# The first gather pass of a two-layer graph network on Trainium2: one-hot rows built from slots that go through DRAM instead of through PE

## The chip, the cores and the metric

The kernel runs on one core of one Trainium2 chip. The metric is the device time of one execution in microseconds. Before the change the median of 3 runs is 19948.8 us (19933.13 to 19953.17).

## The reference, cut to what matters

There are 12500 nodes with 64 features and 412500 edges, sorted by `dst`. The first layer needs, for each edge, the distance between the rows of its two nodes, and the row of its target. What the first gather pass has to produce is, per edge, the product of two rows and their squares:

```python
h = mobius_matvec(weight, input, C)
dist = sqdist(h[edge[0]], h[edge[1]], C)[None, :]   # needs sum(x*y), sum(x*x), sum(y*y) per edge
edge_h = C / (C + dist)
h_e = logmap0(h, C)
...
e_rowsum = jax.ops.segment_sum(edge_e, edge[0], num_segments=N)[:, None]
h_prime = jax.ops.segment_sum(edge_e[:, None] * h_e[edge[1]], edge[0], num_segments=N)
```

`edge[0]` is `src` and `edge[1]` is `dst`. A second layer (edge network, batch norms, sums per node) follows and is not touched.

## The kernel before, in words

**Layout.** The edges are sorted by the kernel itself into tiles of 128, so that all edges of a tile have their `src` node in one chunk of 128 nodes (`ids` holds the chunk of each pair of tiles). A record of 8 floats per edge says the slot of the source node in its chunk (word 0), the target node (word 1) and the attributes. A block is TB = 16 tiles; there are NBLK = 214 blocks, NT = 3424 tiles. The sort (lines 344 to 616) ends with POOL scattering the records to DRAM (L602) while DVE ranks the edges (L495 flags, L503 scans, L508 copies).

**The first gather pass** (lines 754 to 938) works on each block as follows. `each_block` (L779) unrolls four blocks (`g`) in a hardware loop.
- SP loads the records of a block (L821), two buffers, two blocks ahead, after `rec_free` has been given twice: by POOL when it has the indices, and by DVE when it has the slots.
- ACT turns the target nodes into integer indices (`indices`, L848). It does so for block k+2 after the gathers of block k have landed (L851), and it writes the gathered rows to `rows_d` (L853).
- POOL issues 16 indirect DMAs a block (L839), each gathering 128 rows of 68 floats from `h0_d` into `G[g]`, of which there are four.
- The source rows come from a table `T0` in SBUF by a matmul with a one-hot matrix `OT` (slot against partition), per tile (L873). `T0` holds each row as three bf16 pieces of 64 and the three pieces of its square. `OT` needs the slot of each edge on every partition: DVE's `spread` (L900) multiplies the identity by the slots, giving the block's 16 diagonal matrices `DG`; PE's `broadcast` (L867) multiplies them by a matrix of ones into PSUM (`BC`, four banks); DVE's `onehot` (L908) compares `BC` with the partition's number.
- DVE adds the three pieces of the row sums out of PSUM (L919, twice a block, into `xrow` in SBUF) and of the squares (L921), multiplies `xrow` by the gathered rows (L926), copies three words per edge into `EDG` (L927) and sums the products (L930). Then `G[g]` is free.

The order is set by semaphores. The helpers are `consume(eng, s, n)` (L137), a wait followed by a subtraction, `hold` (L110), and `chunks_of` (L130), which loads eight chunk numbers into registers. DVE's order in a block is written out by hand: one-hots of the next block, spread of the one after, reduces, product, copies, sum.

**The second gather pass** (L681 in `gathers`, L689 in `onehots`, product L1359) comes later and isn't touched; it gathers as many rows, from `b_d`.

## Time and profile before

| | us |
|---|---|
| median of 3 runs | 19948.8 |
| the profiled execution's own time | 19907.3 |
| its span, first to last instruction | 19904.8 |
| POOL busy | 12116.0 (61%) |
| DVE busy | 7650.9 (38%) |
| PE busy | 6330.2 (32%) |
| ACT busy | 1873.1 (9%) |
| first gather pass, first to last gather | 5401.8 to 10336.6 |

The profile comes from one execution. Engines are PE (matmuls), PEld (weight loads), DVE (vector), ACT (scalar), POOL (GpSimd) and SP (which only issues DMAs). Busy time leaves out waiting and the issue of DMAs from SP and ACT; an indirect gather issued by POOL counts, since POOL works out its descriptors itself. A row "idle before, releaser" tells how long the engine stood before an instruction and what ended the wait; "issue" means that nothing in the profile was waited for. Lines are those of the kernel before.

### The profile page before, as it was taken

What the parts mean: (1) busy time and instruction counts of PE and PEld (TensorE: products, weight loads), DVE (VectorE), ACT (ScalarE), POOL (GpSimd) and SP (SyncE); (2) the same over time, 40 slices, a digit from 0 to 9 for tenths busy, and PEclk for the clock granted to TensorE, in tenths of its full rate; (3) what the DMA queues carried; (4) which work ended last, traced back from release to release, by engine and by line L of the source; (5) the groups of instructions that cost most, each with busy time, mean ns of one, the idle gap of its engine ahead of it and who ended that gap; (6) DMA issues with size and microseconds to landing.
All of it is one profiled execution on the core that took longest, in us unless ns stands there. A gap on an engine that the chain in (4) does not pass through costs nothing. (4 is left out here: it accounts for less than half of the span.)

```text
span 19904.8 us, 173884 instructions
## 1 busy us (share of the span) xinstructions
PE 6330.2 (32%) x43954; PEld 5014.5 (25%) x44061; DVE 7650.9 (38%) x16776; ACT 1873.1 (9%) x2728; POOL 12116.0 (61%) x12232
## 2 busy tenths in 40 slices
PE   0000000000021211212215744444444444458997
PEld 0000000000010110111105733333333333334885
DVE  5999000000144544544458861111111111226664
ACT  2000000000000000000000001111111111124333
POOL 0388777777677777777756735555555555530442
PEclk6555555555555555555558976666666666668998
DMA  1000000000012222222233311111111111155321
GB/s 49 3 3 2 5 5 5 5 5 5 18 50 52 51 51 53 50 52 50 52 39 98 121 57 40 41 41 40 42 40 41 41 40 42 40 87 189 94 93 54
DMA packets 678218, 917.93 MB, mean 46 GB/s; under 512 B 284316, under 2 KB 431387, under 8 KB 677916
## 3 DMA queue, kind: packets, MB, share of 16 engines
q0 software_dynamic: 322304, 245.26, 8.0%
q1 hardware_dynamic: 294236, 440.78, 7.2%
q10 hardware_dynamic: 61632, 231.44, 3.0%
q14 instruction: 36, 0.29, 0.0%
q8 instruction: 10, 0.16, 0.0%
HBM read 648.03 MB, written 268.67 MB: 46 GB/s over the span
## 5 line engine op out<-in xcount | busy, mean ns | idle before, releaser
L681 POOL DMA_INDIRECT big<-b_d,big x3424 | 3233.4, 944 | 2873.7 <-ACT big L669 1825.9
L602 POOL DMA_INDIRECT rec_d<-big x3224 | 3594.8, 1115 | 1516.1 <-issue 982.7
L839 POOL DMA_INDIRECT big<-h_d,big x3424 | 3763.8, 1099 | 1234.3 <-issue 1007.8
L867 PE MATMUL ps<-big,ones_bc 128*128 128x512 bf16 x750 | 356.4, 622 | 5217.9 <-PEq L140 5016.8
L1359 DVE TENSOR_TENSOR big<-ps,big 128x1024 f32<-128x1024 f32 x214 | 262.0, 1224 | 4450.4 <-PE ps L722 3082.9
L873 PE MATMUL ps<-big 128*128 x3424 | 635.5, 367 | 3504.0 <-PEq L140 1774.0
L722 PE MATMUL ps<-big 128*128 x10272 | 876.5, 213 | 2616.6 <-issue 2615.2
L867 PEld LDWEIGHTS ps<-big,ones_bc 128*128 128x128 bf16 x856 | 93.1, 127 | 5370.6 <-issue 5370.6
L1574 POOL TENSOR_SCALAR big<-iota_f,big 128x128 f32<-128x128 f32 x1070 | 636.6, 613 | 1263.6 <-PE ps L1656 750.0
L873 PEld LDWEIGHTS ps<-big 128*128 128x128 bf16 x3424 | 443.2, 141 | 3806.6 <-issue 3774.2
L722 PEld LDWEIGHTS ps<-big 128*128 128x128 bf16 x10272 | 606.8, 107 | 2838.3 <-issue 2817.5
L623 DVE CAST big<-big 128x896 f32 (+3 forms) x10 | 8.5, 848 | 3397.0 <-DMA big<-h_d 3396.0
L1058 POOL TENSOR_SCALAR big<-iota_f,big 128x128 f32<-128x128 f32 x1070 | 873.5, 827 | 445.9 <-ACT big L1071 227.7
L900 DVE TENSOR_TENSOR big<-ident_b,big 128x2048 bf16<-128x2048 bf16 x214 | 489.9, 2289 | 1485.2 <-DVEq L140 992.1
L1320 PE MATMUL ps<-ident,big 128*128 128x128 f32 x3424 | 958.1, 376 | 156.2 <-PE ps L698 106.0
L1121 PE MATMUL ps<-big 128*128 128x128 f32 x6848 | 818.4, 278 | 319.5 <-DVE big L1058 319.5
L919 DVE TENSOR_REDUCE HA<-ps 128x512 f32<-128x1536 f32 x428 | 752.0, 1757 | 407.4 <-DVEq L140 162.3
L1321 PE MATMUL ps<-big 128*128 128x128 f32 x3424 | 908.0, 360 | 0.0
L1121 PEld LDWEIGHTS ps<-big 128*128 128x128 f32 x6848 | 784.2, 192 | 353.6 <-issue 353.6
L1320 PEld LDWEIGHTS ps<-ident,big 128*128 128x128 f32 x3424 | 787.0, 283 | 204.2 <-issue 204.2
L1656 PE MATMUL ps<-big 128*128 128x64 f32 x6848 | 807.6, 277 | 0.0
L1656 PEld LDWEIGHTS ps<-big 128*128 128x128 f32 x6848 | 801.6, 196 | 0.0
(353 smaller groups left out, 11991.8 us busy)
## 6 DMA issues: line engine op xcount, KB each, us to landing
big<-e_d SPq DMA_DIRECT2D x428, 512.0 KB, 4.5
rows_d<-big ACTq DMA_DIRECT2D x214, 544.0 KB
big<-rows_d SPq DMA_DIRECT2D x214, 544.0 KB, 3.4
e_d<-big ACTq DMA_DIRECT2D x214, 512.0 KB
big<-rec_d SPq DMA_DIRECT2D x858, 64.0 KB, 3.3
big<-h_d,big POOLq DMA_INDIRECT x3424
big<-b_d,big POOLq DMA_INDIRECT x3424
rec_d<-big POOLq DMA_INDIRECT x3224
```

The source lines that it names most:

```text
L602: gp.indirect_dma_start(rec_d, bass.IndirectOffsetOnAxis(ix_stage[b][:, j:j + 1], 0), rec_stage[b][:, j * REC:(j + 1) * REC], None).then_i ...
L681: gp.indirect_dma_start(q.G[b][:, t * q.row:(t + 1) * q.row], None, table, bass.IndirectOffsetOnAxis(q.idx[b][:, t:t + 1], 0)).then_inc(q. ...
L722: m = t.matmul(XSF[:, n * D:(n + 1) * D], lhsT, table[:, ds(c * (3 * D) + s * D, D)], start=(s == 0), stop=(s == 2))
L839: gp.indirect_dma_start(G[g][:, t * ROW:(t + 1) * ROW], None, h0_d, bass.IndirectOffsetOnAxis(idx[g % 2][:, t:t + 1], 0)).then_inc(gath[g] ...
L873: m = t.matmul(XS[h][:, n, 0:3 * D + 3], OT[b][:, (h * HT + n) * P:(h * HT + n + 1) * P], T0[:, ds(chunks[n // 2] * TW, 3 * D + 3)], start ...
L919: v.tensor_reduce(x, XS[h][:, :, 0:3 * D].rearrange("p t (q d) -> p t d q", q=3), AX, ALU.add).then_inc(s_e, 1)
L1058: last = eng.tensor_scalar(u0.O[b][:, n * P:(n + 1) * P], iota_f[:, :], rec4[g][:, n * REC:n * REC + 1], wl[b][:, n:n + 1], ALU.is_equal, ...
L1121: m = t.matmul(ps[:, o:o + P], u0.O[b][:, n * P:(n + 1) * P], G0[g][:, n * ROW:n * ROW + P], start=(n % 2 == 0), stop=(n % 2 == 1))
L1320: t.matmul(o, SUM[b][:, p * P:(p + 1) * P], ident[:, :], start=True, stop=False)
L1321: m = t.matmul(o, watt[:, p * P:(p + 1) * P], recT, start=False, stop=True)
L1574: last = eng.tensor_scalar(u1.O[b][:, n * P:(n + 1) * P], iota_f[:, :], u1.rec[b][:, n * REC:n * REC + 1], None, ALU.is_equal)
L1656: m = t.matmul(ps[:, o:o + D], u1.O[b][:, n * P:(n + 1) * P], MSG[b][:, n * D:(n + 1) * D], start=(n % 2 == 0), stop=(n % 2 == 1))
```

## The change

The slots reach all partitions by DMA instead of by PE. ACT copies the slots of a block to bf16 (`slot`), SP writes them to DRAM in the order of tile and edge (`slots_d`), waits for the landing, reads that row of 2048 values back to all 128 partitions (`SB`), and then loads the records of the block after next. DVE compares `SB` in SBUF. `spread`, `broadcast`, `DG`, `BC` and the matrix of ones are gone. `T0` interleaves each piece of a row with the piece of its square, so one reduce adds 65 sums per edge; there are four reduces of a quarter block, into PSUM. The product reads its row sums from PSUM and writes to SBUF.

```diff
+    slots_d = dram("slots_d", (NBLK, TB * P), BF16)
-        ones_bc = sb("ones_bc", [P, P], BF16)
...
-        T0q = T0w[:, :, 0:3 * D].rearrange("p c (q d) -> p c q d", d=D)
-        T2q = T0w[:, :, 3 * D:3 * D + 3].rearrange("p c (q d) -> p c q d", d=1)
+        T0p = T0w[:, :, 0:3 * (D + 1)].rearrange("p c (q w) -> p c q w", q=3)
+        T0q, T2q = T0p[:, :, :, 0:D], T0p[:, :, :, D:D + 1]
...
-        HT = TB // 2
+        QT = TB // 4
...
+        slot = [take(TB // 2, BF16) for _ in range(2)]
+        SB = [take(TB * P // 2, BF16) for _ in range(2)]
         OT = [take(TB * P // 2, BF16) for _ in range(2)]
-        DG = take(TB * P // 2, BF16)
-        DG3 = DG.rearrange("p (t e) -> p t e", e=P)
-        xrow = HA[:, 2 * NT:2 * NT + TB * D].rearrange("p (t d) -> p t d", d=D)
-        BC = ps[:, 0:TB * P]
-        XS = [ps[:, h * 2048:(h + 1) * 2048].rearrange("p (t w) -> p t w", w=256) for h in (1, 0)]
+        prod = HA[:, 2 * NT:2 * NT + TB * D].rearrange("p (t d) -> p t d", d=D)
+        XS = [ps[:, h * 1024:(h + 1) * 1024].rearrange("p (t w) -> p t w", w=256) for h in range(2)]
+        xrow = ps[:, 2048:2048 + TB * (D + 1)].rearrange("p (t w) -> p t w", w=D + 1)
...
# SP
-                def load(g, i, k, *_):
+                    sp.sem_inc(sb_free[b], 1)
+
+                def spread(g, i, k, last=False, end=False):
                     b = g % 2
-                    consume(sp, rec_free[b], 2)
-                    sp.dma_start(rec[b], rec_blk[ds(k + 2, 1), :, :].rearrange("k p w -> p (k w)")
-                                 ).then_inc(rec_in[b], 16)
+                    consume(sp, slot_rdy[b])
+                    sp.dma_start(slots_d[ds(k, 1), :].rearrange("k (t p) -> p (k t)", p=P), slot[b],
+                                 allow_slow_non_contiguous=True).then_inc(slot_st, 16)
+                    consume(sp, slot_st, 16)
+                    consume(sp, sb_free[b])
+                    sp.dma_start(SB[b], slots_d[ds(k, 1), :].to_broadcast([P, TB * P])).then_inc(sb_in[b], 16)
+                    if not end:
+                        consume(sp, rec_free[b])
+                        sp.dma_start(rec[b], rec_blk[ds(k + 2, 1), :, :].rearrange("k p w -> p (k w)")
+                                     ).then_inc(rec_in[b], 16)
+                each_block(sp, spread)
...
# ACT
-                    a.sem_inc(rec_seen[b], 1)
                     a.activation(idx[b], rec3[b][:, :, 1], ACT.Copy).then_inc(idx_rdy[b], 1)
+                    a.activation(slot[b], rec3[b][:, :, 0], ACT.Copy).then_inc(slot_rdy[b], 1)
...
# PE
+                for h in range(2):
+                    t.sem_inc(xs_free[h], 1)
 
                 def step(g, i, k, last=False, end=False):
...
+                    consume(t, ot_rdy)
+                    chunks = chunks_of(t, k * (TB // 2))
+                    for q in range(4):
+                        consume(t, xs_free[q % 2])
+                        for n in range(QT):
+                            o = q * QT + n
+                            m = t.matmul(XS[q % 2][:, n, 0:3 * D + 3], OT[g % 2][:, o * P:(o + 1) * P],
+                                         T0[:, ds(chunks[o // 2] * TW, 3 * D + 3)], start=True, stop=True)
+                        m.then_inc(xs_rdy[q % 2], 1)
...
# DVE
                 def onehot(b):
-                    consume(v, bc_rdy)
-                    v.tensor_scalar(OT[b], BC, iota_p[:, 0:1], None, ALU.is_equal).then_inc(ot_rdy, 1)
+                    consume(v, sb_in[b], 16)
+                    v.tensor_scalar(OT[b], SB[b], iota_p[:, 0:1], None, ALU.is_equal).then_inc(s_oh, 1)
+                    consume(v, s_oh)
+                    v.sem_inc(ot_rdy, 1)
+                    v.sem_inc(sb_free[b], 1)
 
                 def step(g, i, k, last=False, end=False):
                     if not last:
                         onehot((g + 1) % 2)
-                    if not end:
-                        spread(g % 2)
...
+                    for q in range(4):
+                        consume(v, xs_rdy[q % 2])
+                        v.tensor_reduce(xrow[:, q * QT:(q + 1) * QT, :],
+                                        XS[q % 2][:, :, 0:3 * D + 3].rearrange("p t (q w) -> p t w q", q=3), AX, ALU.add
                                         ).then_inc(s_e, 1)
...
+                        v.wait_ge(s_e, q + 1)
+                        v.sem_inc(xs_free[q % 2], 1)
                     consume(v, g_rdy[g])
-                    v.tensor_tensor(xrow, xrow, G3[g][:, :, 0:D], ALU.mult).then_inc(s_e, 1)
+                    v.tensor_tensor(prod, xrow[:, :, 0:D], G3[g][:, :, 0:D], ALU.mult).then_inc(s_e, 1)
                     v.tensor_copy(EDG3[:, ds(k * TB, TB), :], G3[g][:, :, SQ:SQ + 3]).then_inc(s_e, 1)
+                    v.tensor_copy(X2A[:, ds(k * TB, TB)], xrow[:, :, D]).then_inc(s_e, 1)
...
+                    v.tensor_reduce(XY[:, ds(k * TB, TB)], prod, AX, ALU.add).then_inc(s_e, 1)
```

## Rows read from the trace of the kernel before

**Rows 1.** The page, POOL's busy tenths in 40 slices of 498 us.

```profile
POOL 0388777777677777777756735555555555530442
```

**Rows 2.** First pass: stretch, us, busy us per engine (instructions), granted clock, DMA share, GB/s.

```profile
5401.00:10337.00 4936.00, 991.74 (x4174) 536.28 (x4280) 2320.43 (x1923) 48.79 (x213) 3763.84 (x3424) 0.51 0.23 51
```

**Rows 3.** The gathers L839, as a group, and their durations (ns, min/median/max).

```profile
L839 POOL DMA_INDIRECT big<-h_d,big x3424 | 3763.8, 1099 | 1234.3 <-issue 1007.8 <-POOLq L140 226.4
...
L839 POOL DMA_INDIRECT big<-h_d,big x3424: 940/944/3053, 5401.8 to 10335.7; - x191
```

**Rows 4.** Timeline of two ordinary blocks: start us, us, instruction, idle before.

```profile
7000.55 0.23 ACT L848 ACTIVATE big<-big 128x16 int32<-128x16 f32 x1 [21.11 <-ACTq L140]
7000.61 2.29 DVE L900 TENSOR_TENSOR big<-ident_b,big 128x2048 bf16<-128x2048 bf16 x1 [8.56 <-DVEq L140]
7001.06 2.66 POOL L839 DMA_INDIRECT big<-h_d,big  x1 [0.30 <-issue]
...
7005.57 1.76 DVE L919 TENSOR_REDUCE HA<-ps 128x512 f32<-128x1536 f32 x1 [0.26 <-DVE HA L921]
...
7006.52 0.94 POOL L839 DMA_INDIRECT big<-h_d,big  x1 [0.30 <-issue]
...
7007.68 1.23 DVE L926 TENSOR_TENSOR HA<-HA,big 128x1024 f32<-128x1024 f32 x1 [0.26 <-DVE HA L921]
...
7007.77 1.94 POOL L839 DMA_INDIRECT big<-h_d,big  x1 [0.30 <-issue]
...
7010.72 2.35 DVE L908 TENSOR_SCALAR big<-ps,iota_p 128x2048 bf16<-128x2048 f32 x1 [0.26 <-DVEq L140]
7011.27 0.94 POOL L839 DMA_INDIRECT big<-h_d,big  x1 [0.30 <-issue]
...
7023.75 2.65 POOL L839 DMA_INDIRECT big<-h_d,big  x1 [0.30 <-issue]
```

**Rows 5.** The second gather pass: its gathers' durations, and its product's group.

```profile
L681 POOL DMA_INDIRECT big<-b_d,big x3424: 938/944/1037, 11923.7 to 17762.2; - x191
...
L1359 DVE TENSOR_TENSOR big<-ps,big 128x1024 f32<-128x1024 f32 x214 | 262.0, 1224 | 4450.4 <-PE ps L722 3082.9
```

**Rows 6.** Waits of POOL in the first pass: us in total, times, longest us.

```profile
POOL big L839 <- POOLq L140: 226.4, 153, 63.3
```

**Rows 7.** Timeline: one of the halts of the first pass.

```profile
6438.15 2.35 DVE L908 TENSOR_SCALAR big<-ps,iota_p 128x2048 bf16<-128x2048 f32 x1 [29.42 <-issue]
...
6463.54 0.94 POOL L839 DMA_INDIRECT big<-h_d,big  x1 [12.53 <-POOLq L140]
```

**Rows 8.** The sort: two widths of compare L495, and its timeline beside POOL's scatters.

```profile
L495 DVE TENSOR_SCALAR big<-HA,iota_f 128x1612 bf16<-128x1612 bf16 x99 | 63.2, 639 | 0.1
...
L495 DVE TENSOR_SCALAR big<-HA,iota_f 128x248 bf16<-128x248 bf16 x99 | 27.9, 283 | 0.0
...
1701.35 1.95 DVE L508 COPY_PREDICATED big<-big 128x1612 f32<-128x1612 uint16 x1
1702.39 1.71 POOL L602 DMA_INDIRECT rec_d<-big  x1 [0.30 <-issue]
...
1703.34 0.64 DVE L495 TENSOR_SCALAR big<-HA,iota_f 128x1612 bf16<-128x1612 bf16 x1
```

**Rows 9.** The narrow compares of the second gather pass, durations.

```profile
L689 DVE TENSOR_SCALAR big<-iota_b,big x3424: 234/248/517, 11923.1 to 17723.2; 128x128 bf16<-128x128 bf16 x191
```

**Rows 10.** DMA queues from 203 to 226 us: the store of h_d, 40 slices.

```profile
DMA  0099999999999999999999999999989999894000
```

**Rows 11.** Timeline: SP issues the ids' store, waits for it and issues their load.

```profile
614.19 0.35 SPq L409 DMA_DIRECT2D ids_d<-big  x1
...
615.63 0.23 SPq L411 DMA_DIRECT2D ids<-ids_d  x1
```

**Rows 12.** The page's DMA issues: KB each, us to landing.

```profile
big<-e_d SPq DMA_DIRECT2D x428, 512.0 KB, 4.5
```

**Rows 13.** DVE's last reduce in the first pass: busy us, mean ns of one.

```profile
L930 DVE TENSOR_REDUCE HA<-HA 128x1024 f32 x212 | 258.6, 1220 | 49.5 <-DVE big L927 31.8 <-issue 17.8
```

More of the change, by code:

```diff
@@ L766, in build @@
         idx = [take(TB, I32) for _ in range(2)]
+        slot = [take(TB // 2, BF16) for _ in range(2)]
+        SB = [take(TB * P // 2, BF16) for _ in range(2)]
         OT = [take(TB * P // 2, BF16) for _ in range(2)]
-        DG = take(TB * P // 2, BF16)
-        DG3 = DG.rearrange("p (t e) -> p t e", e=P)
-        xrow = HA[:, 2 * NT:2 * NT + TB * D].rearrange("p (t d) -> p t d", d=D)
-        BC = ps[:, 0:TB * P]
-        XS = [ps[:, h * 2048:(h + 1) * 2048].rearrange("p (t w) -> p t w", w=256) for h in (1, 0)]
+        prod = HA[:, 2 * NT:2 * NT + TB * D].rearrange("p (t d) -> p t d", d=D)
+        XS = [ps[:, h * 1024:(h + 1) * 1024].rearrange("p (t w) -> p t w", w=256) for h in range(2)]
+        xrow = ps[:, 2048:2048 + TB * (D + 1)].rearrange("p (t w) -> p t w", w=D + 1)
         two = lambda k: [sem(f"l0_{k}{b}") for b in range(2)]
-        rec_in, rec_seen, rec_free, idx_rdy = two("rec"), two("recseen"), two("recfree"), two("idx")
+        rec_in, rec_free, idx_rdy, slot_rdy, sb_in, sb_free = (
+            two(k) for k in ("rec", "recfree", "idx", "slot", "sb", "sbfree"))
         gath, g_rdy, g_free, stored = ([sem(f"l0_{k}{g}") for g in range(4)] for k in ("gath", "grdy", "gfree", "stored"))
         xs_rdy, xs_free = two("xs"), two("xsfree")
-        s_dg, dg_rdy, bc_rdy, ot_rdy, s_e = (sem(f"l0_{k}") for k in ("spread", "dg", "bc", "ot", "e"))
+        s_oh, ot_rdy, s_e, slot_st = (sem(f"l0_{k}") for k in ("oh", "ot", "e", "slotst"))
         def each_block(eng, body):
@@ L816, in _ @@
                     sp.dma_start(rec[b], rec_blk[b]).then_inc(rec_in[b], 16)
-                def load(g, i, k, *_):
+                    sp.sem_inc(sb_free[b], 1)
+                def spread(g, i, k, last=False, end=False):
                     b = g % 2
-                    consume(sp, rec_free[b], 2)
-                    sp.dma_start(rec[b], rec_blk[ds(k + 2, 1), :, :].rearrange("k p w -> p (k w)")
-                                 ).then_inc(rec_in[b], 16)
-                with sp.Fori(0, NBLK // 4) as i:
-                    for g in range(4):
-                        load(g, i, i * 4 + g)
+                    consume(sp, slot_rdy[b])
[9 more added lines that the diff above has]
+                each_block(sp, spread)
             @block.gpsimd
@@ L895, in _ @@
             def _(v):
-                v.memset(ones_bc[:, :], 1.0).then_inc(s_e, 1)
-                def spread(b):
-                    consume(v, rec_seen[b])
-                    v.tensor_tensor(DG3, ident_b[:, :].unsqueeze(1).to_broadcast([P, TB, P]),
-                                    bcast(rec3[b][:, :, 0], P), ALU.mult).then_inc(s_dg, 1)
-                    consume(v, s_dg)
-                    v.sem_inc(dg_rdy, 1)
-                    v.sem_inc(rec_free[b], 1)
-                def onehot(b):
-                    consume(v, bc_rdy)
-                    v.tensor_scalar(OT[b], BC, iota_p[:, 0:1], None, ALU.is_equal).then_inc(ot_rdy, 1)
+                def onehot(b):
+                    consume(v, sb_in[b], 16)
[3 more added lines that the diff above has]
+                    v.sem_inc(sb_free[b], 1)
                 def step(g, i, k, last=False, end=False):
```

44 lines of the change are left out of this document (3 added, 41 removed).

## The prediction

> **What bounds the kernel now.** I read four views in this order. The page's slices [rows 1] place the first gather pass: it fills slices 12 to 20 of the 40, in which POOL stands at 7 tenths. The window of that pass [rows 2] gives POOL 3763.8 us of 4936.0, against 2320.4 for DVE and 991.7 for PE, so nothing but POOL is near full. The groups [rows 3] show that all of POOL's work is 3424 indirect gathers (L839, 214 blocks of 16 tiles), mean 1099 ns, and that its idle time is almost all "issue", POOL's own step from one gather to the next. The range of durations [rows 3] is the hint: median 944 ns, longest 3053. So 3763.8 - 3424 x 0.944 = 531.5 us are spent in gathers that take longer than they need to.
>
> The timeline of two ordinary blocks [rows 4] says which. At 7001.06 a gather begins inside the spread (L900, 7000.61 to 7002.90) and lasts 2.66 us; it ends 0.82 us after the spread does. At 7007.77 one begins inside the product (L926, ends 7008.91), lasts 1.94 us and ends 0.80 us after it. Gathers under the two wide reduces from PSUM (L919) and under the one-hot compare from PSUM (L908) take 0.94 us. The next block repeats it (2.65 at 7023.75). L900 and L926 are the two wide DVE instructions of the pass with two inputs in SBUF. Per block that is 1.7 + 0.9 to 1.0 = 2.6 to 2.7 us; 214 blocks would give some 560, and 531.5 is the total, so this is nearly all of the excess. The second gather pass is a control: its DVE product (L1359) reads one side from PSUM, and its 3424 gathers have mean 944 ns, longest 1037 [rows 5].
>
> POOL's ledger for the pass: 3424 x 0.944 = 3232 us of plain gathers, 531.5 of held ones, and 1234.3 idle, of which 63.3 lie before the first gather [rows 3, 6] and 3423 x 0.304 = 1040 are the steps between gathers. 131 us are left; those are halts like the one of 12.53 us at 6463.54 [rows 7], where DVE's compare had stood still for 29 us shortly before, the records were reloaded late, and POOL ran out of indices.
>
> **The change, part by part.**
> *Spread (L900) and product.* L900 goes. The product now takes its row sums from PSUM, so it has one SBUF input, the form of L1359. Removed: 531.5 us of held gathers. Nothing hides this, since POOL runs back to back.
>
> *The one-hot compare.* It read PSUM as f32 at 2351 ns; now it reads bf16 from SBUF. The same form in the sort (L495) took 639 ns for 1612 elements and 283 for 248, slope 0.261 ns, so 2048 elements take about 0.75 us [rows 8]. Does it hold POOL? In the sort's timeline a gather-like scatter starts at 1702.39 inside a two-input instruction that ends 1703.30 and ends itself at 1704.10, 0.80 later, although a 0.64 us compare ran from 1703.34 to 1703.98 meanwhile [rows 8]. In the second pass 3424 narrow compares of this form left the gathers at 944 [rows 5] but were themselves up to 517 ns long against 248 [rows 9]: there DVE was the one that waited. So the cost per block lies between 0 and its own length, 0.75 us (161 us in all; a gain is excluded, the gathers of today's compare are at 944 already). I take 0.2 us, nearer the rows: 43 us.
>
> The Trainium skill, "SBUF — State Buffer", section "Who interferes with whom", says that whichever of a DVE tensor_scalar in a two-port mode and a GpSimd instruction starts first keeps the other out entirely; by that alone the compare costs up to the 161 us. The sort's scatter shows no such addition, the narrow compares show the half in which DVE waits.
>
> *The way through DRAM on SP.* Per block SP now waits for the slots, writes them, waits for the landing, reads them back broadcast, and only then reloads the records. The write has 16 x 128 = 2048 pieces of two bytes. No row has such a piece. Nearest rows: the store of h_d, 128 x 99 = 12672 rows of 272 bytes, kept the engines busy for 35 of 40 slices of 0.575 us, 20 us [rows 10], 25 ns for each of an engine's 792 rows; 128 pieces an engine at that price are 3.3 us. The store of the ids (128 pieces of 56 bytes) had landed 1.44 us after issue, when SP went on [rows 11]. Sum 4.7 us; bounds 1.5 us (pieces free) and 11 us (three times the price). The broadcast read moves 512 KB into SBUF, as each load of e_d does: 4.5 us to landing [rows 12]. SP is thus occupied some 5 to 7 us of a 20 us block, and the compare's input is there some 12 us after the block begins, 8 before POOL is at its end. I cost this at nothing; what hides it is POOL's 20 us. Without that cover (a write of more than about 18 us) SP sets the block. The record reload moves behind both transfers, but it waits for rec_free, which POOL gives when it starts the block; its indices are wanted 20 us later. ACT gets a second 0.23 us copy per block, with over 20 us idle around it [rows 4]. The transfers share the DMA engines, now 23% busy [rows 2], with the gathers; a gather that lands a few us later delays only indices with a block in hand.
>
> The Trainium skill speaks against this part: "DMA: Bandwidth & Descriptors", section "Rules for kernel authors", has one descriptor per element for a strided last dimension and advises rearranging. The estimate from a figure of "VectorE: DVE Perf Modes", section "The three transpose paths" (19 times 1309 ns for 128x128) is 24.9 us for 16384 elements, 3.1 us for 2048, like the sum from the rows.
>
> *DVE and PE.* DVE per block: 0.75 (compare), four reduces of 780 elements (L919 took 1.76 for 1536 [rows 4], so at most about 1.0 each, 3.9 in all), product 1.22, two small copies some 0.3, last reduce 1.22 [rows 13]: 7.4 us, with its waits about 10 of 20. Before it was 2320.4 / 214 = 10.8 [rows 2]. The handshakes with PE go from two to four a block; PE loses the four broadcast matmuls. Neither is the bound: 0, covered by POOL.
>
> *Halts.* DVE no longer frees the records. It frees the slot rows instead, two blocks deep, so a DVE that is 30 us late should reach POOL less often. But PE and DVE meet more often. I keep half of 131: 65 us saved (bounds: all 131, or none).
>
> *Sum.* 531.5 - 43 + 65 = 553 us off the profiled execution's 19907.3, which stands 41.5 under the median of the runs: 19948.8 - 553 = 19396.
>
> **Rivals.**
> 1. *The compare takes over the hold* (16%): each block loses the full 0.75 us, and no halt is saved. 19948.8 - 531.5 + 161 = 19578. For it: it is an SBUF to SBUF instruction at four elements a cycle. Against it: rows 8 and 9.
> 2. *SP becomes the bound* (5%): a write of two-byte pieces at 200 ns each would be 25.6 us, with 2 us of issue 27.6 per block against 22.6 now, 214 x 5 = 1070 us more: 21019. It decides from 160 ns a piece, where SP's cycle passes today's 22.6 [rows 4]; the row of h_d gives 25. Between 18 and 22.6 us a block is a smaller gain (3%).
> 3. *The hold is not the two inputs* (2%). Then long gathers stay: 19949, and with the compare's 161 on top 20110. The same page of the skill, "SBUF — State Buffer", same section, infers that a tensor_tensor takes only the read side and descriptor generation needs the write side, so that L900 could not hold a gather; by that rule nothing is returned. The gathers that end 0.82 and 0.80 us behind L900 and L926 contradict it.
> 4. *The change does not do what it says* (1%): if the compare fell back to one element a cycle it would be 2.3 us, which DVE has to spare. Same as the forecast.
>
> **How the numbers follow.** The forecast's case has 73%. Its own range is 19285 (531.5 and 131 saved, compare free) to 19578 (rival 1's sum); I reach a little past that for a compare that also costs a landing or two, to 19600. About 0.2%, 40 us, is what a measurement of this kernel can tell from no change. Faster 0.92 (forecast, rivals 1 and 4, the small gain of 2), same 0.02, slower 0.06.
>
> **What the new profile would show.** POOL's gathers at median 944 and mean 950 to 975 ns, none of 2.6 us; the block period near 20.2 us where it was 22.6; a compare of 0.75 us; the slot write landing in 3 to 7 us; POOL's wait for indices no longer than today's. Wrong: a mean above 1000 ns (rival 1 or 3), POOL idle behind ACT with SP's queue in the write's wait in every block (rival 2), or a pass that ends more than 200 us from 4380 us after its first gather (4271 of gathers and steps, 43, 66).

## The result and the profile after

The changed kernel takes 20233.5 us (median), the kernel before 19942.1 beside it: ratio 1.0139, 95% interval 1.0119 to 1.0158. One of the four executions behind the median took 22002 us, at a granted clock of 0.554 where the others had 0.61, and the ratio leaves it out. I had forecast 19396 and given "slower" 6%. The profiled execution took 20230.6, with a span of 20228.8.

The table below splits the two spans at the first and last starts of the gathers of both passes.

| us | before | after | difference |
|---|---|---|---|
| start to first gather of the first pass | 5401.8 | 5411.2 | +9 |
| first pass | 4933.9 | 5197.4 | +264 |
| between the passes | 1588.0 | 1656.2 | +68 |
| second pass | 5838.5 | 5839.9 | +1 |
| to the end | 2142.6 | 2124.1 | -18 |

So the pass that was to get 553 us shorter got 264 us longer; I did not follow the 68 behind it. The groups of the page that answer to [rows 3] and [rows 5], with the changed kernel's DVE instructions (the first column is busy us and mean ns, the second idle us before them and who ended most of it):

```profile
L681 POOL DMA_INDIRECT big<-b_d,big x3424 | 3242.6, 947 | 2867.0 <-ACT big L669 1817.0
...
L846 POOL DMA_INDIRECT big<-h_d,big x3424 | 3255.6, 951 | 2005.9 <-issue 1341.2
...
L900 DVE TENSOR_REDUCE ps<-ps 128x260 f32<-128x780 f32 x856 | 837.8, 979 | 1614.1 <-DVEq L140 951.9
...
L890 DVE TENSOR_SCALAR big<-big,iota_p 128x2048 bf16<-128x2048 bf16 x214 | 164.5, 769 | 1966.5 <-DMA big<-slots_d 758.8
```

The hold is gone: busy time of the gathers fell from 3763.8 to 3255.6 us, 508 us, and the mean from 1099 ns to 951. The idle time before them rose from 1234.3 to 2005.9, 772 us. The gain was made and more than given back as waiting. Two rows say where to look: DVE stood 1614 us before its reduces of PE's results, and 1966.5 us before its compare, of which 758.8, the largest part, is put down to `slots_d`. The first pass in the view of [rows 2]:

```profile
5400.00:10600.00 5200.00, 694.79 (x3384) 368.36 (x3384) 1551.81 (x1906) 74.91 (x428) 3248.25 (x3417) 0.50 0.75 70
```

The DMA engines' busy share went from 0.23 to 0.75. The granted TensorE clock is 0.50, the lower of its levels (1.2 GHz), as before (0.51), so the clock isn't the difference in this pass. The timeline of one block, the SyncE queue and the instructions that matter (start us, us, instruction, idle before):

```profile
7007.72 1.40 SPq L827 DMA_DIRECT2D big<-slots_d  x1
...
7011.40 0.98 DVE L900 TENSOR_REDUCE ps<-ps 128x260 f32<-128x780 f32 x1 [10.29 <-issue]
...
7014.02 1.40 SPq L830 DMA_DIRECT2D big<-rec_d  x1
...
7015.10 0.95 POOL L846 DMA_INDIRECT big<-h_d,big  x1 [3.47 <-issue]
...
7020.43 0.73 SPq L823 DMA_DIRECT2D slots_d<-big  x1
...
7034.52 1.40 SPq L827 DMA_DIRECT2D big<-slots_d  x1
...
7040.77 0.23 ACT L854 ACTIVATE big<-big 128x16 int32<-128x16 f32 x1 [27.01 <-DMA big<-rec_d]
...
7040.87 0.73 SPq L830 DMA_DIRECT2D big<-rec_d  x1
...
7046.21 0.17 DVE L908 COPY HA<-ps 128x16 f32 x1
...
7047.32 0.95 POOL L846 DMA_INDIRECT big<-h_d,big  x1 [12.34 <-POOLq L140]
```

SP writes the slots at 7020.43 and can issue the read back at 7034.52, 14 us later; over the pass this gap is 16.1 us in the median, and 12.8 to 19.1 in nine blocks of ten. Then come the read, the record reload at 7040.87, and only then the next write: the cycle is 26.8 us here and 24.3 in the mean, while POOL needs 20 for a block. ACT stands 27 us for records, POOL 3.47 us for indices. So rival 2, given 5%, looked like the answer. It was one of two. The second shows in the last two rows: POOL's next block has its indices at 7041.0, made by the ACT instruction above, and yet starts only at 7047.32, behind DVE's copy at 7046.21, after which DVE gives the row buffer back. There it is a late DVE that ends the halt.

### The profile page after: what moved, and what is told of

It reads as the page before. It is cut to its first block and busy times, and to the rows that moved or that the text cites. A ratio compares the mean times of both kernels' runs of the same rounds, so it can differ in the third digit from the quotient of the medians.

```text
span 20228.8 us, 174633 instructions
## 1 busy us (share of the span) xinstructions
PE 6011.3 (30%) x43204; PEld 4824.0 (24%) x43205; DVE 6921.2 (34%) x16775; ACT 1899.6 (9%) x2942; POOL 11622.1 (57%) x12232
## 5 line engine op out<-in xcount | busy, mean ns | idle before, releaser
L846 POOL DMA_INDIRECT big<-h_d,big x3424 | 3255.6, 951 | 2005.9 <-issue 1341.2
L881 PE MATMUL ps<-big 128*128 x3424 | 703.1, 364 | 9348.8 <-PEq L140 6929.5
L881 PEld LDWEIGHTS ps<-big 128*128 128x128 bf16 x3424 | 372.7, 131 | 9679.1 <-issue 9656.8
L722 PE MATMUL ps<-big 128*128 x10272 | 875.7, 213 | 2627.1 <-issue 2626.7
L900 DVE TENSOR_REDUCE ps<-ps 128x260 f32<-128x780 f32 x856 | 837.8, 979 | 1614.1 <-DVEq L140 951.9
L722 PEld LDWEIGHTS ps<-big 128*128 128x128 bf16 x10272 | 605.4, 107 | 2850.6 <-issue 2828.3
L1098 PEld LDWEIGHTS ps<-big 128*128 128x128 f32 x6848 | 782.5, 192 | 388.4 <-issue 388.4
L890 DVE TENSOR_SCALAR big<-big,iota_p 128x2048 bf16<-128x2048 bf16 x214 | 164.5, 769 | 1966.5 <-DMA big<-slots_d 758.8
L1633 PEld LDWEIGHTS ps<-big 128*128 128x128 f32 x6848 | 795.0, 195 | 0.0
L1298 PEld LDWEIGHTS ps<-big 128*128 128x128 f32 x3424 | 764.4, 275 | 0.0
L503 DVE TENSOR_TENSOR_SCAN big<-big 128x248 f32<-128x248 bf16 (+3 forms) x396 | 749.0, 1891 | 0.1
```

Source lines behind the costliest of these rows:

```text
L503: v.tensor_tensor_scan(scn[c % 2][:, 0:w], f, f, cur[:, c:c + 1], ALU.add, ALU.max).then_inc(s_count, 1)
L722: m = t.matmul(XSF[:, n * D:(n + 1) * D], lhsT, table[:, ds(c * (3 * D) + s * D, D)], start=(s == 0), stop=(s == 2))
L846: gp.indirect_dma_start(G[g][:, t * ROW:(t + 1) * ROW], None, h0_d, bass.IndirectOffsetOnAxis(idx[g % 2][:, t:t + 1], 0)).then_inc(gath[g] ...
L881: m = t.matmul(XS[q % 2][:, n, 0:3 * D + 3], OT[g % 2][:, o * P:(o + 1) * P], T0[:, ds(chunks[o // 2] * TW, 3 * D + 3)], start=True, stop= ...
L900: v.tensor_reduce(xrow[:, q * QT:(q + 1) * QT, :], XS[q % 2][:, :, 0:3 * D + 3].rearrange("p t (q w) -> p t w q", q=3), AX, ALU.add).then_ ...
L1098: m = t.matmul(ps[:, o:o + P], u0.O[b][:, n * P:(n + 1) * P], G0[g][:, n * ROW:n * ROW + P], start=(n % 2 == 0), stop=(n % 2 == 1))
```

## A fact that has to stand ahead of the experiments

The chips on which these kernels ran fall into two groups. On one the kernel before takes 19821 to 19942 us (medians of 19942, which is the 19949 of the prediction with one execution more, 19821, 19905 and 19881), on the other 18310 to 18342 (18320, 18341, 18342, 18310). I call them the 19.9 ms and the 18.3 ms chips. Most of the difference can be placed in a pass that no experiment touches, the second gather pass, which has the same idle time in every kernel on one group and another on the other. The group of its gathers, in the kernel before as the prediction had it, then in the changed kernel on an 18.3 ms chip:

```profile
L681 POOL DMA_INDIRECT big<-b_d,big x3424 | 3233.4, 944 | 2873.7 <-ACT big L669 1825.9
```

```profile
L681 POOL DMA_INDIRECT big<-b_d,big x3424 | 3236.8, 945 | 1392.5 <-issue 1088.4
```

That is 1481 us of some 1600. Gathers, POOL's steps and DVE instructions last the same on both. PE's do not: this is the group of its matmuls L722 in that pass, in the same two runs.

```profile
L722 PE MATMUL ps<-big 128*128 x10272 | 876.5, 213 | 2616.6 <-issue 2615.2
```

```profile
L722 PE MATMUL ps<-big 128*128 x10272 | 491.3, 195 | 3.4 <-issue 3.3
```

On a 19.9 ms chip PE stands 2616.6 us before these matmuls, waiting for nothing that the profile shows, and on an 18.3 ms chip 3.4. The granted clock over the second pass is 0.62 and 0.68, a mix of its two levels. In the first pass it is 0.50 or 0.51 on both (0.50 in e6c and in e6, the same kernel), so there it doesn't tell the groups apart. What differs there: on the 19.9 ms chips DVE stands for results whose matmuls, by the trace, ended long before, and SP's own steps often take 0.7 us.

## The experiments

The table gives all of them by chip. "Pass" is busy plus idle of the gathers' group, less the 63 us ahead of the first; "DVE" is the idle time before its reduces of PE's results. In the kernel before and in the e3 runs the compare waits for PE as well: its idle time is 610 us in before, 194 in b2, 1984 in e3e and 84 in e3d.

| kernel | chip's before | time | ratio (interval) | gathers' mean ns | POOL idle | pass | DVE |
|---|---|---|---|---|---|---|---|
| before | 19948.8 | | | 1099 | 1234.3 | 4935 | 407 |
| b2, before | 19820.6 | 19815.8 | | 1107 | 1139.4 | 4866 | 225 |
| after | 19942.1 | 20233.5 | 1.0139 (1.0119 to 1.0158) | 951 | 2005.9 | 5198 | 1614 |
| a2, after | 19820.6 | 20414.5 | 1.0305 (1.0271 to 1.0340) | 948 | 2164.1 | 5346 | 981 |
| e5 | 19820.6 | 20006.8 | 1.0090 (1.0062 to 1.0118) | 959 | 1774.2 | 4993 | 3206 |
| e6c | 19905.1 | 19977.0 | 1.0034 (1.0021 to 1.0046) | 976 | 1687.9 | 4965 | 3248 |
| e3e | 19881.2 | 20157.8 | 1.0145 (1.0128 to 1.0162) | 967 | 1933.9 | 5182 | 709 |
| a3, after | 18341.6 | 18187.4 | 0.9923 (0.9905 to 0.9942) | 953 | 1423.7 | 4622 | 260 |
| e1 | 18320.1 | 17859.2 | one run | 953 | 1136.8 | 4337 | 260 |
| e1b | 18341.4 | 17892.3 | one run | 953 | 1139.9 | 4340 | 260 |
| e2 | 18320.1 | 17888.7 | 0.9759 (0.9743 to 0.9776) | 955 | 1145.2 | 4354 | 260 |
| e4 | 18320.1 | 17933.2 | one run | 956 | 1192.8 | 4402 | 260 |
| e6 | 18341.4 | 17911.3 | 0.9769 (0.9753 to 0.9785) | 962 | 1128.0 | 4360 | 150 |
| e6b | 18341.6 | 17913.0 | 0.9760 (0.9744 to 0.9776) | 961 | 1128.4 | 4356 | 150 |
| e7 | 18341.4 | 18211.9 | one run | 982 | 1352.3 | 4652 | 150 |
| e7b | 18341.6 | 18177.2 | 0.9907 (0.9887 to 0.9927) | 982 | 1347.2 | 4648 | 150 |
| e3 | 18320.1 | 17925.0 | 0.9780 (0.9764 to 0.9797) | 982 | 1120.1 | 4419 | 151 |
| e3b | 18341.4 | 17958.8 | 0.9790 (0.9773 to 0.9806) | 982 | 1122.2 | 4420 | 151 |
| e3c | 18341.6 | 17943.0 | 0.9777 (0.9760 to 0.9793) | 982 | 1121.8 | 4421 | 151 |
| e3d | 18310.5 | 17935.2 | 0.9789 (0.9772 to 0.9805) | 979 | 1119.4 | 4409 | 151 |

### e1, e2: the write in one piece

```diff
-                    sp.dma_start(slots_d[ds(k, 1), :].rearrange("k (t p) -> p (k t)", p=P), slot[b],
-                                 allow_slow_non_contiguous=True).then_inc(slot_st, 16)
+                    sp.dma_start(slots_d[ds(k, 1), :].rearrange("k (p t) -> p (k t)", p=P), slot[b]).then_inc(slot_st, 16)
```

This permutes the slots within a block. e2 takes the permutation up by a read of PE that goes through the one-hot in steps of 16 columns: `OT[g % 2].rearrange("q (e t) -> q t e", t=TB)[:, o, :]`.

> The changed kernel with the slots written to DRAM as 32 contiguous bytes per partition (128 pieces) where it was 2048 pieces of two bytes. The order of the slots in DRAM is then edge before tile, and nothing else is adapted, so the one-hot rows (and the first layer's distances) are computed from permuted slots; the work is the same. Theory A (the two-byte pieces: the write holds SP for 15.6 us, and SP's 24.4 us per block set the pass): the write lands in about 2 us, SP's cycle falls to 9 to 12 us, POOL's 20 us per block bound again, the pass takes 4300 to 4400 us where it took 5198, total 19350 to 19450 us. Rival B (PE's handshakes with DVE, which came up to 12 us late in 203 of 844 cases, delay DVE, and through the freed slot rows SP and POOL): four handshakes a block are unchanged, so the pass stays at 5000 to 5200 us, total 20050 to 20230. Rival C (SP's own slow steps, 0.7 us each, some 8.7 us a block) alone would not be enough to pass 20 us and gives the same as A.

> As e1, and the matmuls take their one-hot weights with a step of 16 elements, so that the result is the reference's again. Theory A: as e1, 19350 to 19450 us, if the weight loads with a step stay below 1 us each (16 of them a block, 20 us of cover). If such a load takes over 1 us, PE with its waits becomes the bound and the total rises by 214 us for each us per block above 20. Rival B: 20050 to 20230.

SyncE's queue in e1b, a repeat of e1:

```profile
7017.92 0.36 SPq L823 DMA_DIRECT2D slots_d<-big  x1
7020.28 0.33 SPq L826 DMA_DIRECT2D big<-slots_d  x1
7020.88 0.33 SPq L829 DMA_DIRECT2D big<-rec_d  x1
```

Write to read back is 2.36 us, against 18.7 in the changed kernel on such a chip (a3, below). The pass falls to 4337 us: of POOL's 1137 us of idle time in e1 63 lie ahead of it and 1040 are the steps, so 34 are left. The kernel is 2.4% faster than before (e2). The stepped read of PE costs nothing: 30 us between e1 and e2, near the 0.2% that a measurement tells.

### e3: the kernel before, its spread in narrow pieces

```diff
-                    v.tensor_tensor(DG3, ident_b[:, :].unsqueeze(1).to_broadcast([P, TB, P]),
-                                    bcast(rec3[b][:, :, 0], P), ALU.mult).then_inc(s_dg, 1)
+                    for t in range(TB):
+                        last = v.tensor_scalar(DG[:, t * P:(t + 1) * P], ident_b[:, :], rec[b][:, t * REC:t * REC + 1],
+                                               None, ALU.mult)
+                    last.then_inc(s_dg, 1)
```

> The kernel before with one part changed: the spread of a block is 16 tensor_scalar instructions of 128 columns (one tensor input and a scalar per partition) in place of one tensor_tensor of 2048 with two SBUF inputs. No DRAM trip. The product keeps its two SBUF inputs. Theory H (two SBUF inputs hold the gathers): 1.7 us per block are returned, the product's 0.9 stay: mean of the gathers from 1099 to about 1000 ns, total 19942 - 364 = 19580, 19540 to 19640. Rival (any wide DVE work on SBUF holds them, or the narrow ones in their fast mode do): mean stays above 1060 ns, total 19900 or more, and above 20000 if each of 16 holds a gather by 0.25 us.

It is 395 us faster on this chip, and 375 to 399 in three repeats on chips of the group. My working from [rows 4] was 1.7 us per block for L900's hold, 364 us. The gathers' mean is 982 ns, 38 over the plain 944; 3424 of them make 130 us, which is left to the product, less than the 0.9 to 1.0 us a block, some 200 us, of my working. The narrow pieces are also much shorter than the spread, so this run by itself doesn't tell two inputs from length; that the changed kernel's compare (0.75 us), its product from PSUM and its last reduce (1.22 us each) hold next to nothing does. With both, the first half of the prediction stands: the hold comes from the wide DVE instructions with two SBUF inputs, and it goes with them.

### e4: the record reload moved ahead of the landing

```diff
-    sp.dma_start(slots_d[ds(k, 1), :].rearrange("k (t p) -> p (k t)", p=P), slot[b],
+    sp.dma_start(slots_d[ds(k, 1), :].rearrange("k (t p) -> p (k t)", p=P), slot[g],
                  allow_slow_non_contiguous=True).then_inc(slot_st, 16)
-    consume(sp, slot_st, 16)
-    consume(sp, sb_free[b])
-    sp.dma_start(SB[b], slots_d[ds(k, 1), :].to_broadcast([P, TB * P])).then_inc(sb_in[b], 16)
     if not end:
         consume(sp, rec_free[b])
         sp.dma_start(rec[b], rec_blk[ds(k + 2, 1), :, :].rearrange("k p w -> p (k w)")
                      ).then_inc(rec_in[b], 16)
+    consume(sp, slot_st, 16)
+    consume(sp, sb_free[b])
+    sp.dma_start(SB[b], slots_d[ds(k, 1), :].to_broadcast([P, TB * P])).then_inc(sb_in[b], 16)
```

`slot` has four buffers for it, since indices run further ahead.

> The changed kernel with the records of block k+2 reloaded between the issue of the slot write and the wait for its landing (four slot buffers instead of two); the two-byte pieces stay. Theory A1 (SP's cycle as a whole is the bound): SP still waits the 15 us of the landing in each block, its cycle stays at 21 to 24 us, total 19700 to 20230. Rival A2 (only the place of the reload behind the landing starves POOL): POOL finds its records in time, block 20.2 us, total 19350 to 19450.

The write still lands late, and now costs little. Its SyncE queue:

```profile
7012.28 0.41 SPq L823 DMA_DIRECT2D slots_d<-big  x1
7012.94 3.73 SPq L827 DMA_DIRECT2D big<-rec_d  x1
...
7032.14 0.33 SPq L831 DMA_DIRECT2D big<-slots_d  x1
7033.46 0.41 SPq L823 DMA_DIRECT2D slots_d<-big  x1
```

19.9 us from write to read back, a cycle of 20.6 us in the mean, pass 4402, against 4622 in a3 and 4337 in e1. So most of what the write costs here isn't that the slots arrive late, they are wanted a block later, but that SP stands in the wait with the next block's records behind it.

### b2, a2, e5: on a 19.9 ms chip

e5 is e2 and e4 together: wide write, early reload.

> The kernel before, unchanged, to have its profile on the chip of these runs; the first profile came from a chip on which it took 19942 us, the second chip of the study took 18320. If this is a chip like the second: first pass 4271 + 531 us of held gathers = 4800 to 4850, no late handshakes between PE and DVE, total 18320. If like the first: 4930, total 19940.

> The changed kernel, unchanged. Theory A (SP's cycle with the two-byte pieces is the bound on every chip): the pass takes over 5000 us again and the kernel is slower than before by 1 to 2%. Theory D (the chip matters: where PE's completions reach DVE at once, as on the second chip, the two-byte write is nearly hidden): pass 4400 to 4600 us, total 1.2 to 2.2% under before on a chip like the second, and 1.4% over before only on one like the first.

> Contiguous slot write, weights taken with a step of 16, and the reload ahead of the wait for the landing: the two edits of e2 and e4 together. If SP is no longer the bound after either, nothing is added: the same as e2 within 30 us (pass 4300 to 4400). If the two add up, 50 us or more under e2.

The loss repeats, and at 1.0305 it is larger than the 1 to 2% expected. e5 takes 353 us off the pass against a2 and is still 0.9% slower than before; its pass of 4993 us is far from the 4300 to 4400 expected. So the write is not all. Its DVE waits (us in total, times, longest us):

```profile
DVE ps L900 <- remote: 1366.6, 159, 10.9
DVE ps L900 <- DVEq L140: 961.9, 351, 10.9
DVE ps L900 <- issue: 831.3, 198, 10.9
```

DVE stands 3206 us before its reduces, hundreds of times up to 10.9 us, on PE, which is busy a seventh of the pass. The timeline of the changed kernel shows one:

```profile
6990.00 0.83 PE L881 MATMUL ps<-big 128*128 x4 [16.19 <-issue]
...
6991.19 0.83 PE L881 MATMUL ps<-big 128*128 x4 [0.36 <-issue]
...
7000.13 0.98 DVE L900 TENSOR_REDUCE ps<-ps 128x260 f32<-128x780 f32 x1 [9.29 <-DVEq L140]
...
7001.45 0.83 PE L881 MATMUL ps<-big 128*128 x4 [9.43 <-PEq L140]
...
7011.40 0.98 DVE L900 TENSOR_REDUCE ps<-ps 128x260 f32<-128x780 f32 x1 [10.29 <-issue]
```

Two buffers take turns. The matmuls at 6990.00 fill the first, those at 6991.19 the second, and these end at 6992.02. DVE empties the first buffer at 7000.13, and PE fills it anew at 7001.45. The reduce at 7011.40 reads the second: it waits for nothing but matmuls that by the trace ended 19.4 us earlier. (DVE had nothing else to do: its last instruction had ended 10.29 before.) In this run 207 reduces waited more than 1 us, and they started 15.8 us after the end of their own matmuls in the median, 23.1 at most. I took this for a fault of the new quarter buffers, which give PE too little lead to hide it.

### e6, e7: half-block buffers

```diff
-        QT = TB // 4
-        xrow = ps[:, 2048:2048 + TB * (D + 1)]
+        QT = TB // 2
+        xrow = HA[:, 2 * NT + TB * D:2 * NT + TB * D + TB * (D + 1)]
-                    for q in range(4):
+                    for q in range(2):
```

e6 is e5 with this, e7 the changed kernel with this alone. The product reads two SBUF inputs again.

> The wide write and the early reload of e5_wide_reload_first, and TensorE's results in half-block buffers again: two pairs of handshakes with VectorE per block in place of four, the row buffer of the sums back in SBUF (so the product of a half block reads two SBUF inputs again). Theory (beneath SyncE's cycle it is TensorE's completions that reach VectorE late, and quarter buffers, each used twice per block, leave no lead to hide that): the late arrivals are hidden again, the hold of the product comes back at about 0.9 us per block (190 us), first pass near 4520 us, total about 350 us under the kernel before on the same chip. Rival (SyncE's cycle of 23 us, whose steps are slow in themselves, is the bound however the buffers are cut): pass near 5000 us, total at or above the kernel before.

> The changed kernel with half-block buffers alone; the two-byte write and the place of the reload stay. If SyncE's cycle (24 to 25 us per block, two thirds of it the wait for the two-byte write to land) is a cause that stands by itself: pass near 5200 us and a total over 1.5% above the kernel before. If only the late completions of TensorE matter: a landing wait that shrinks to the 12.5 us of the quickest ones, pass under 4900 us, total under the kernel before.

> The changed kernel with one contiguous write for the slots (their order is permuted in the block; nothing else is adapted to it), as in e1_wide_write, run again beside the kernels of this call. If the two-byte write is the whole of the loss: pass near 4350 us, total some 500 us under the kernel before. If TensorE's late completions bind beneath it: pass near 5000 us, total within 1.5% of the kernel before.

> The kernel before with its spread as 16 narrow products, as in e3_narrow_spread, run again beside the kernels of this call: no DRAM write, half-block buffers, only the hold of the product left. Theory: the held half of the gathers' excess goes whatever the chip does with handshakes: 360 to 400 us under the kernel before (1.9%). Rival (on a chip where handshakes come late, VectorE's own time becomes the bound once POOL is quicker): less than 150 us.

These four fell on an 18.3 ms chip. There e6 is no better than e2 (0.9769 against 0.9759; the product's hold costs 63 us over 944 ns a gather, not the 190 I expected), and e7, whose write is still in two-byte pieces, keeps the cycle of 21.7 us and a pass 292 us longer than e6's; it is 0.7% faster than before. What I expected of it was worked out for a 19.9 ms chip and can't be judged here. The write, with the reload behind it, costs 280 to 350 us of pass in every pair: e7 over e6, a3 over e1b (282, two chips of the group), a2 over e5 (353, with SP's slow steps). In the first and the last pair the place of the reload changes too.

### a3, e6b, e3c, e7b: the change itself on an 18.3 ms chip

> The changed kernel as it is. The kernel before takes 18.3 ms on some chips and 19.8 to 19.9 ms on others. If the gathers of this call show the first kind (before near 18330 us): theory, the SyncE cycle of e7_halves_alone (21.7 us per block) with the same landing time and two handshakes more per block, 18150 to 18250 us, so some 0.5 to 1% faster than before; rival, the change loses on every chip, over 18450 us. If the second kind (before near 19820 us): again 1.5 to 3% slower, 20150 to 20450 us.

> As e6_wide_halves. On a chip of the first kind (before near 18330 us) again 17911 us within 50. On a chip of the second kind: theory (half-block buffers hide the late completions), pass near 4500 us and 250 to 400 us under before; rival (SyncE's slow steps bind by themselves), pass near 5000 us and a total at or above before.

> As e3_narrow_spread: on a chip of the first kind again 2.1% under before. On the second kind: theory, no write to DRAM and the late completions hidden by the half blocks, so 250 to 400 us under before; rival, VectorE's own time (4.5 us more per block) becomes the bound where its handshakes come late, less than 150 us under before.

> As e7_halves_alone: the two-byte write and its place, with half-block buffers. On a chip of the first kind again 18212 us (0.7% faster). On the second kind it shows what the write costs where the late completions are hidden: theory of two stacked causes, SyncE's cycle of 24 us or more stays and the total is at or above before; rival (the late completions are the whole of the loss), pass under 4800 us and at least 100 us under before.

The changed kernel is 0.8% *faster* here. Its groups:

```profile
L846 POOL DMA_INDIRECT big<-h_d,big x3424 | 3261.9, 953 | 1423.7 <-issue 1024.7
...
L900 DVE TENSOR_REDUCE ps<-ps 128x260 f32<-128x780 f32 x856 | 837.7, 979 | 259.8 <-DVEq L140 255.5
```

Busy time as in the first run; but 582 us less idle, and DVE waits 0.3 us before a reduce, never more than 0.45. SyncE's queue of one block:

```profile
7000.81 0.41 SPq L823 DMA_DIRECT2D slots_d<-big  x1
...
7019.48 0.33 SPq L827 DMA_DIRECT2D big<-slots_d  x1
7020.07 0.33 SPq L830 DMA_DIRECT2D big<-rec_d  x1
...
7020.66 0.41 SPq L823 DMA_DIRECT2D slots_d<-big  x1
```

The landing is even later here (18.7 us; over the pass 20.0 in the median, 18.2 to 23.6 in nine blocks of ten), but SP goes on 0.6 us per step, so its cycle is the landing and little more, 21.6 us. The DMA engines in this pass, forty slices:

```profile
DMA  9999999999999999999999999999999999999999
```

In e1b they stand at 3. The gathers have as many packets in both kernels, but over this stretch their queue has 54.1% of the engines' time with the two-byte write and 17.2% without: 2048 tiny pieces a block slow everything that shares the engines.

Is it this traffic that makes the landing late? The first block of the pass says: not in the main. Its write and its read back, and the DMA engines from 5404 to 5407 us, 40 slices of 0.075 us:

```profile
5404.15 0.42 SPq L823 DMA_DIRECT2D slots_d<-big  x1
...
5422.02 0.37 SPq L827 DMA_DIRECT2D big<-slots_d  x1
```

```profile
DMA  0000000000000003877777777777776420099900
...
q1 hardware_dynamic: 2064, 0.00, 30.7%
```

The 2048 pieces have gone through by 5406.5, 2.3 us after the issue, before all but the first two gathers. SP waits for nothing but the landing (the read's buffer is free from the start), and it can issue the read only 17.9 us after the write. So some 15 us of it lie between the last piece's packet and the signal of the landing, and a busy pass adds 2 us in the median.

### e6c: the wide write with half blocks, on a 19.9 ms chip

> As e6_wide_halves. On a chip where the kernel before takes near 18330 us: again 17911 us within 50. On a chip where it takes near 19820 us: theory (half-block buffers hide the late completions), pass near 4500 us and 250 to 400 us under before; rival (SyncE's slow steps bind by themselves), pass near 5000 us and a total at or above before.

1.0034. The half blocks hid nothing. The same group of this kernel, first on this chip, then on an 18.3 ms chip:

```profile
L900 DVE TENSOR_REDUCE HA<-ps 128x520 f32<-128x1560 f32 x428 | 762.9, 1782 | 3248.4 <-remote 1475.3
```

```profile
L900 DVE TENSOR_REDUCE HA<-ps 128x520 f32<-128x1560 f32 x428 | 762.9, 1782 | 149.7 <-DVEq L140 149.7
```

With two handshakes in place of four the total wait is the same (3206 in e5): each is now twice as long. The reduces that waited more than 1 us started 39.2 us (median) after the end of their own eight matmuls; in e5 it was 19.5 after their own four. My theory of the quarter buffers falls.

### e3d, e3e: the same question without any part of the change

> As e3_narrow_spread. On a chip where the kernel before takes near 18330 us: again 2.1 to 2.2% under before. On a chip where it takes 19800 to 19950 us: theory (what loses there is the changed order of work between TensorE and VectorE and the write; this kernel has neither), the held half of the excess goes, 250 to 400 us under before, with few late completions of TensorE. Rival (the held gathers hide a rhythm of such a chip that binds at 22 to 23 us per block, whatever is released): late completions in many blocks, within 0.5% of before.

> As e3_narrow_spread: where the kernel before takes near 18330 us, 2.1% under before. Where it takes 19800 to 19950 us: theory (the loss there belongs to the changed order of work), 250 to 400 us under before with few late completions of TensorE; rival (a rhythm of 22 to 23 us per block binds there once gathers are no longer held), late completions in many blocks and within 0.5% of before.

e3d fell on an 18.3 ms chip again. e3e is the run that tells most. It is the kernel before in everything but the narrow spread: no DRAM write, the old buffers, the broadcast by PE. On four chips of 18.3 ms it gains 2.1 to 2.2%; on this one it is 1.45% slower than before, which is worse than the rival's 0.5% too. Its groups, and one block of its timeline:

```profile
L839 POOL DMA_INDIRECT big<-h_d,big x3424 | 3311.2, 967 | 1933.9 <-issue 1037.6
...
L910 DVE TENSOR_SCALAR big<-ps,iota_p 128x2048 bf16<-128x2048 f32 x214 | 503.1, 2351 | 1984.2 <-DVEq L140 1025.5
```

```profile
7037.19 1.49 PE L867 MATMUL ps<-big,ones_bc 128*128 128x512 bf16 x3 [8.31 <-PEq L140]
...
7066.25 2.35 DVE L910 TENSOR_SCALAR big<-ps,iota_p 128x2048 bf16<-128x2048 f32 x1 [26.76 <-DVEq L140]
...
7072.39 0.70 SPq L821 DMA_DIRECT2D big<-rec_d  x1
...
7074.12 0.23 ACT L848 ACTIVATE big<-big 128x16 int32<-128x16 f32 x1 [45.55 <-ACTq L140]
...
7077.50 0.18 DVE L929 COPY big<-big 128x48 f32 x1
...
7078.62 0.94 POOL L839 DMA_INDIRECT big<-h_d,big  x1 [12.36 <-POOLq L140]
```

PE's broadcast ends at 7038.68 (the trace has three of its four matmuls here; the same lateness shows in the blocks where it has all four). DVE's compare needs that and nothing else, and starts 27.6 us later. Behind it stands the spread, which frees the records; behind that SP's reload and ACT's indices, at 7074.12. POOL, which halts 12.36 us, takes these and then still waits for its row buffer, which DVE gives back only after its copy at 7077.50. This comes about every third block: 71 of the compares start over 20 us after the broadcast's end, nearly all of them 27 to 29 us. The picture is that of [rows 7], halt and all. On an 18.3 ms chip the same L910 is 84.0 us idle in the whole pass (e3d).

## Why the prediction was wrong

**The hold: right.** 531.5 us were in gathers held by L900 and L926; after, 3424 gathers are 23 us over 944 ns each. The compare holds nearly nothing: I took 43 us for it, bounds 0 to 161, and 23 is all the excess there is, which refutes rival 1. With the wide two-input instructions out, the long gathers are gone (the longest takes 1453 ns, where it was 3053), which refutes rival 3. What the Trainium skill infers under "Who interferes with whom" ("SBUF — State Buffer"), that a tensor_tensor can't keep descriptor generation out, does not hold here; e3 removed one such instruction per block, and on each of the four 18.3 ms chips 375 to 399 us came back, where 1.7 us a block are 364. The same item there has a tensor_tensor with both inputs in SBUF contend with what GpSimd reads; these gathers read their indices from SBUF, and with that half the traces agree.

**"I cost this at nothing; what hides it is POOL's 20 us": wrong.** Write to landing was 4.7 us by my sum, 11 at most. From the write to the read back it is 16.1 us in the median, and 20.0 in a3 on an 18.3 ms chip. I priced a piece from the store of h_d, 25 ns for 272 bytes on an engine. That was no underestimate for the pieces: in the first block of a3 they are through 2.3 us after the issue. What the sum had at nothing are the 15.5 us from there to the signal of the landing. The one landing that I went by, the store of the ids after 1.44 us [rows 11], had 128 pieces; e1's write, with 128 too, has landed after 2.4 us. Why 2048 pieces take so long to be reported no run shows. I had the deciding point right (SP's cycle over about 18 us is a smaller gain) and gave that variant 3%; on the 18.3 ms chips it is what happened: forecast by my sum -553, measured -154, and with the wide write -449 (e1b). The Trainium skill's rule for strided last dimensions ("DMA: Bandwidth & Descriptors", "Rules for kernel authors") spoke against the write, and the runs agree with it; the estimate worked out from the transposes' figure, 3.1 us, was as far off as mine. The second half of this step was what SP is moved past. I counted the reload's wait for rec_free and not that the reload is late when the landing is: e4 shows that this, more than the landing, makes the loss (220 of 285 us of pass on the 18.3 ms chips).

**"The handshakes go from two to four a block. Neither is the bound: 0": wrong on the chip at hand, and the profile held signs of it.** I compared busy times, 7.4 us of DVE against 20, and halts of 131 us. But [rows 5] held 3082.9 us of DVE standing for PE's L722 in the second pass, whose gathers are not held; POOL was idle 2873.7 us there, 1825.9 of it behind ACT (the group shown above, which I had in the page and did not read). I now read that pass as a picture of the first one with its hold removed. The first pass's idle time did rise towards it on the 19.9 ms chips (from 1139 and 1234 us to between 1688 and 2164, against some 2870), but that one cause makes both is not shown. And [rows 7] showed the mechanism: a DVE that is 29 us late, then a halt of POOL. I priced it at what it cost while gathers were slow, and forecast a saving of 65.

**What the time is made of, then.** On the 19.9 ms chip: -508 us held gathers, +772 idle. By pairs, the two-byte write with the reload behind it is some 200 to 350 us (after or a2 against e5). The rest goes with the late results: e5, e6c and e3e have no two-byte write, gathers within 32 ns of plain, and still passes of 4965 to 5182, as long as or longer than the held one. Whatever releases POOL there, it waits instead. Had I sized the write rightly I would still have been wrong on this chip; on the others the hold's mechanism was right and the write's term was the largest error: with it mended (e1b) 449 of the 553 us are there. The other 104 can't be placed, since the kernel before has no trace on such a chip; the 65 us of halts saved may be among them.

**Open.** Why PE's results reach DVE late on some chips I can't say. It isn't the buffers (e6c), the write (e5, e3e) or the handshakes' number, and it isn't the granted clock of the first pass. One rival stands: that nothing is wrong with the signal, and PE itself works slowly there. Two things speak for it. The lateness grows with the work: 19.5 us in the median behind four matmuls of 195 columns (e5) and 39.2 behind eight (e6c). And in the second pass PE stands 2616.6 us before its own L722 matmuls, for nothing that the profile shows, where it stands 3.4 on an 18.3 ms chip. No run separates the two, since the ends of matmuls in the trace are modelled. Nor do I know why the kernel before has few late results in this pass (DVE idle 407 and 225 us before its reduces, 610 and 194 before its compare) and e3e so many (709 and 1984); that the held gathers spread things out is a guess. Not run: the kernel before on an 18.3 ms chip with its trace kept, and e2 or e4 on a 19.9 ms chip.

## What to carry to other kernels

Removing what slows the bounding engine pays only down to the next rhythm, so look in the same profile for a sibling stage that already runs without it: if that one idles, this one may too. A transfer in tiny pieces is priced by a measured landing of one with as many pieces, not by their time on the engines, and most of what it costs is the queue behind its landing wait: move the reload ahead of the wait, and write wide, with the permutation taken up by a strided read of PE (e2: 30 us at most, and 2.4% won). Time a change on more than one chip before believing its sign: this one is 0.8% faster or 1.4 to 3.1% slower, while e2's form was among the best on one group (e6 equals it) and nothing that I ran on the other beats the kernel before.

## What the runs showed that I hadn't expected

- Chips differ by up to 9% on this program (18310 to 19942 us) with equal durations of gathers and DVE instructions. Most of the difference is in the second pass, where PE stands 2616.6 us before L722 on one group and 3.4 on the other.
- On the slower ones DVE goes on up to 23.1 us (after), 43.5 us (e6c) and 28.8 us (e3e's broadcast) after the end of the matmuls it waits for, as the trace models it. On the others DVE is never idle for more than 0.45 us before a reduce (a3, e6).
- SyncE's steps differ too: its issues of the read back, min/median/max ns, in the changed kernel on a 19.9 ms and on an 18.3 ms chip:

```profile
L827 SPq DMA_DIRECT2D big<-slots_d x214: 2/699/1408, 5426.2 to 10645.7; - x107
```

```profile
L827 SPq DMA_DIRECT2D big<-slots_d x214: 256/333/370, 5422.0 to 10073.7; - x107
```

- In a3's first block 2048 pieces of two bytes are through 2.3 us after the issue and reported as landed after 17.9.
- 2048 pieces of two bytes a block took the DMA engines from 0.3 to 0.9 busy and the gathers' queue from 17.2% of their time to 54.1%, for 4 KB.
